# An attention layer on one core: new slot table with gaps, other order of the first steps, later clears, an earlier end of the last groups

## The chip, the cores and the metric

The kernel runs on one core of one Trainium2 chip. The metric is device time of one execution in microseconds. Engines are called by name: TensorE (PE in the rows, PEld for its weight loads), VectorE (DVE), ScalarE (ACT), GpSimd (POOL), SyncE (SP, which issues the DMAs). L12 is line 12 of the kernel.

## The reference, cut to what matters

```
x: (8, 1024, 256); 16 heads of 16; c = softplus(log_c); beta = softplus(beta)
h = layernorm(x);  q, k, v = h @ W.T, each mapped to the Poincare ball (exp_map)
dist = arccosh(max(1 + 2c*|q-k|^2 / ((1-c|q|^2)(1-c|k|^2)), 1+EPS)) / sqrt(c)
w = softmax(-beta*dist - bias);  o = w @ log_map(v);  o = log_map(exp_map(o))
x = x + o @ W_o.T
x = x + bf16(fp8_gemm(bf16(layernorm(x)), kernel)) + bias
```

Nearly all of the work is the 8 x 16 x 1024 x 1024 distances: a logarithm and a power of each.

## The kernel before, in words

**Tiles.** The 8192 tokens are 16 groups of 512 queries (G; in the tables the number n). Each group (counted from 0) takes 32 steps (`STEPS`): 4 sets of four heads, and in each 8 key tiles of 128. So n runs over 512 steps. A step has, on TensorE, the distances of four heads (`distances`, L1081; its two halves belong to two different coming steps) and the weights times values (`values`, L1096); on ScalarE a logarithm of 128x2048 numbers out of PSUM (Ln, L1192) and an exponential (Exp, L1199, the power of the step before). `distances(n + 1, second)` waits until Ln of step n has freed the shared banks. U is a ring of four buffers.

**Two paths.** Every unit of four steps reads a flag in a register and takes one of two branches. In the rare one VectorE bounds and clamps first (L1259, L1268) and Ln works on the result (L1187). In this data three units do, in groups 5, 8 and 15.

**The work between.** Projections of coming groups and the finish of past ones are cut into pieces and put into steps by a table written by hand. All pieces share PSUM bank 7: TensorE fills it, VectorE copies it out, and the next piece waits for that. `PROJECT_USES` and `FINISH_USES` say in which slot a piece stands and in which half: 0 (before `values`), 1 (after) or BOTH (split around it). Kinds: X turns the normalised input, M is a projection (four rows of L398 each), R turns scaled rows of queries or keys, A the largest values for the flags; T, W turn the attention's output and multiply it by W_o, Q and Y are the 8-bit product. S, every eighth step from step 10 (`SUM_STEPS`), turns the sums and has VectorE normalise them (L1282 to L1286). For groups from 3 on, slot k stands in step k - 4; for group 2 (`SECOND_USES`) in step k of group 0; for group 1, `FIRST_USES` names the steps of group 0. The finish of a group stands in the next group, the last but one uses `SHORT_USES`. VectorE's own arithmetic has slots too (`vector`, with its counts in `OWN`).

**Unread products.** A step with no piece gets two products (L1119, `keep_busy`) that nobody reads, one in each half.

**Start.** Groups 0 and 1 are projected before the loop through six PSUM banks (`FIRST_FILLS`); ScalarE copies. `first_vector` does VectorE's part for both. GpSimd clears `rows` and part of `vals` (`pool_zero`).

**End.** After the last step `last_tensor`, `last_scalar`, `last_vector` finish the last group. Then VectorE works out whether the fast path held; a flag is summed on TensorE and copied; after the block every engine loads it into a register and branches around the general path, which this data doesn't take.

## Time and profile before

| | us |
|---|---|
| three runs | 2004.28, 2000.06, 1993.87 |
| median | 2000.06 |
| profiled execution | 2002.46 |
| its span | 2000.7 |
| ScalarE busy | 1874.2 (94%) |
| TensorE busy | 1804.3 (90%) |
| VectorE busy | 1140.0 (57%) |
| mean granted TensorE clock | 0.972 |

Instructions of one engine overlap a little, so that 512 Ln and Exp of 1.92 and 1.96 us take less than their sum. The distance between the starts of two Ln is the length of a step.

### The profile page before, as it was taken

What the parts mean: (1) busy time and instruction counts of PE and PEld (TensorE: products, weight loads), DVE (VectorE), ACT (ScalarE), POOL (GpSimd) and SP (SyncE); (2) the same over time, 40 slices, a digit from 0 to 9 for tenths busy, and PEclk for the clock granted to TensorE, in tenths of its full rate; (3) what the DMA queues carried; (4) which work ended last, traced back from release to release, by engine and by line L of the source; (5) the groups of instructions that cost most, each with busy time, mean ns of one, the idle gap of its engine ahead of it and who ended that gap; (6) DMA issues with size and microseconds to landing.
All of it is one profiled execution on the core that took longest, in us unless ns stands there. A gap on an engine that the chain in (4) does not pass through costs nothing.

```text
span 2000.7 us, 29621 instructions
## 1 busy us (share of the span) xinstructions
PE 1804.3 (90%) x10753; PEld 609.2 (30%) x10753; DVE 1140.0 (57%) x2825; ACT 1874.2 (94%) x1094; POOL 14.5 (1%) x35
## 2 busy tenths in 40 slices
PE   7988989999898798989998898998989899999997
PEld 4222322323232232322322232232323223333334
DVE  7463565655566665665657656555655656322545
ACT  5789999999999699999998899999999999999992
POOL 2000000000000000000000000000000000000000
PEclk9699999999999899999999899999999999999997
DMA  1314113131312213122040320414122131311110
GB/s 56 111 68 124 54 64 96 38 133 43 112 43 81 73 43 112 44 100 75 22 133 22 102 74 24 131 43 133 40 94 65 43 102 44 122 43 43 43 33 22
DMA packets 112952, 142.53 MB, mean 71 GB/s; under 512 B 35691, under 2 KB 61548, under 8 KB 112748
## 3 DMA queue, kind: packets, MB, share of 16 engines
q1 hardware_dynamic: 112748, 140.13, 21.8%
q8 instruction: 89, 1.46, 0.3%
q14 instruction: 115, 0.94, 0.2%
HBM read 85.07 MB, written 55.05 MB: 70 GB/s over the span
## 4 chain that ended last, share of the span: by engine, by line
ACT 47%; PE 32%; issue 13%; DVE 5%; ACTq 3%; DMA 0%; DVEq 0%; SPq 0%
ACT U L1192 25%; ACT U L1199 22%; PE ps L1081 10%; PE ps L398 9%; PE ps L1096 8%; PE ps L688 3%; ACTq L1240 2%; DVE U L1268 1%; PE ps L1119 1%; DVE U L1259 1%; PE ps L403 0%; DMA U<-in_L_attn_W_o_dram 0%; DVE ss L532 0%; PE ps L394 0%; PE ps L168 0%
## 5 line engine op out<-in xcount | busy, mean ns | idle before, releaser
L1199 ACT ACTIVATE U<-U 128x2048 f32<-128x2048 f32 x512 | 1002.6, 1960 | 0.3
L1192 ACT ACTIVATE U<-ps 128x2048 f32<-128x2048 f32 x500 | 961.3, 1923 | 37.8 <-PE ps L1081 31.1
L1081 PE MATMUL ps<-q_T,k_T 18*128 18x512 f32 x4096 | 632.9, 650 | 133.5 <-ACT U L1192 108.1
L1096 PE MATMUL ps<-U,vals 128*32 128x512 f32 x4096 | 561.2, 620 | 27.6 <-ACT U L1199 27.3
L1081 PEld LDWEIGHTS ps<-q_T,k_T 18*128 18x128 f32 x4096 | 196.8, 186 | 349.3 <-ACT U L1192 270.4
L398 PE MATMUL ps<-wT,xnT 128*128 128x384 f32 x512 | 230.9, 543 | 4.8 <-DVEq L1292 2.5
L487 DVE COPY qkv<-ps 128x384 f32<-128x384 f32 x112 | 62.5, 558 | 221.0 <-PE ps L398 221.0
L1119 PE MATMUL ps<-woT,ident 128*128 128x256 f32 x396 | 141.7, 441 | 0.0
L1096 PEld LDWEIGHTS ps<-U,vals 128*32 128x32 f32 x4096 | 81.5, 109 | 197.5 <-ACT U L1199 133.6
L398 PEld LDWEIGHTS ps<-wT,xnT 128*128 128x128 f32 x512 | 80.7, 192 | 196.6 <-issue 112.1
L495 DVE COPY q_T<-ps 128x512 f32<-128x512 f32 x60 | 41.5, 692 | 124.3 <-PE ps L403 124.3
L403 PE MATMUL ps<-ident,rows 128*128 128x128 f32 x512 | 108.3, 308 | 3.3 <-DVEq L1292 1.7
L403 PEld LDWEIGHTS ps<-ident,rows 128*128 128x128 f32 x512 | 55.0, 146 | 181.1 <-issue 133.1
L1119 PEld LDWEIGHTS ps<-woT,ident 128*128 128x128 f32 x396 | 60.5, 192 | 162.3 <-issue 147.8
L1274 DVE COPY OTs<-ps 128x512 f32<-128x512 f32 x64 | 43.8, 684 | 73.1 <-PE ps L1096 73.1
L497 DVE COPY k_T<-ps 128x512 f32<-128x512 f32 x60 | 41.5, 692 | 70.7 <-PE ps L403 70.5
L688 PE MATMUL ps<-woT,fi_ocT 128*128 128x256 f32 x240 | 67.8, 405 | 0.0
L1282 DVE TENSOR_REDUCE den<-ps 128x16 f32<-128x256 f32 x64 | 27.2, 424 | 70.4 <-PE ps L1105 69.8
L688 PEld LDWEIGHTS ps<-woT,fi_ocT 128*128 128x128 f32 x240 | 40.6, 189 | 51.0 <-issue 25.2
L578 DVE TENSOR_REDUCE ss<-sqr 128x48 f32<-128x768 f32 x56 | 53.4, 953 | 1.9
L716 DVE TENSOR_TENSOR fi_x<-fi_xt,ps 128x512 f32<-128x512 f32 x30 | 20.6, 688 | 57.1 <-PE ps L688 57.1
L577 DVE TENSOR_TENSOR sqr<-qkv 128x768 f32<-128x768 f32 x56 | 53.1, 948 | 0.0
(209 smaller groups left out, 1177.8 us busy)
## 6 DMA issues: line engine op xcount, KB each, us to landing
rqb<-q_scratch SPq DMA_DIRECT2D x64, 1024.0 KB, 5.6
q_scratch<-q_T SPq DMA_DIRECT2D x16, 1024.0 KB, 4.5
k_scratch<-k_T SPq DMA_DIRECT2D x16, 1024.0 KB, 6.8
v_scratch<-vals SPq DMA_DIRECT2D x16, 768.0 KB, 9.5
fi_xt<-in_L_attn_x_dram SPq DMA_DIRECT2D x17, 512.0 KB, 5.2
xt<-in_L_attn_x_dram SPq DMA_DIRECT2D x15, 512.0 KB, 6.0
out_dram<-fi_x SPq DMA_DIRECT2D x15, 512.0 KB, 3.4
rk_scratch<-rk SPq DMA_DIRECT2D x16, 32.0 KB, 11.5
```

The lines of the kernel that those rows point to most:

```text
L398: ins = pe.matmul(bank[:, 0:384], xnT[:, dc, t * P:(t + 1) * P], g.wT[:, dc, half * 384:(half + 1) * 384], start=dc == 0, stop=dc == 1)
L403: ins = pe.transpose(bank[:, t * P:(t + 1) * P], rows[:, qk, t, hg * HPG:(hg + 1) * HPG, :].rearrange("p h r -> p (h r)"), g.ident[:, :])
L487: v.tensor_copy(qkv[:, t, 24 * half:24 * (half + 1), :].rearrange("p h d -> p (h d)"), bank[:, 0:384]).then_inc(a.b7_copied, 1)
L577: step(v.tensor_tensor(sqr[:, :], src, src, ALU.mult))
L578: step(v.tensor_reduce(ss[:, t, :], sqr[:, :].rearrange("p (h d) -> p h d", d=DH), AX.X, ALU.add))
L688: ins = pe.matmul(bank[:, a * D:(a + 1) * D], ocT[:, dc, t * P:(t + 1) * P], g.woT[:, dc, :], start=dc == 0, stop=dc == 1)
L1081: ins = pe.matmul(g.ps[:, 2 * pair + i, :], a.k_T[HB * h:HB * h + RD, b % 2, hg, kt * P:(kt + 1) * P], a.q_T[HB * h:HB * h + RD, G % 3, hg ...
L1096: ins = pe.matmul(g.ps[HB * h:HB * h + VW, 6, :], a.vals[:, b % 2, kt, (hg * HPG + h) // 2, DH * (h % 2):DH * (h % 2) + VW], U[:, n % RING ...
L1119: pe.matmul(g.ps[:, 7, 0:D], g.ident[:, :], g.woT[:, 0, :], start=True, stop=True)
L1192: act.activation(U[:, n % RING].rearrange("p b n -> p (b n)"), chunk(n), ACT.Ln, scale=-2.0 / EPS, bias=1.0).then_inc(freed, 1)
L1199: act.activation(U[:, n % RING], U[:, n % RING], ACT.Exp, scale=exponent).then_inc(exp_done, 1)
L1274: v.tensor_copy(OTs[:, :], g.ps[:, 6, :]).then_inc(ot_done, 1)
```

## The change

- **Table.** M4 to M7 move one slot back, so that slots 11 and 14 are empty; the pieces T, W of the finish move one slot back and W1 two (T 13, 14; W 15, 17). VectorE's slots from the third sum of squares on move one back, as does the projection's small exponential on ScalarE (slot 20 to 21); so do the finish's from 20 on. Step 7 (`BARE`) gets no unread products.
- **Group 2.** R pieces stand in 25 to 31 instead of 24 to 31.
- **First steps.** In step 0 TensorE waits for the last start copy and does five unread products. A0, R4, A1 of group 1 stand in that order in step 2, half 0. R7 and R0 stand in steps 11 and 14. VectorE scales only group 1's keys before the loop and its queries in step 3.
- **Clears.** GpSimd waits for VectorE's first normalised input, and clears only the part of `rows` that is not written later.
- **Last two groups.** `SHORT_SLOTS` packs the finish of group 14: Q in step 25, Y0 and Y1 in step 27, the residual in 28, the store in 29. Before: Q 27, Y 28, residual 29, store 30. The last group's transposes get eleven unread products after them instead of eight.
- **Flag.** VectorE's four operations of the flag stand after its copy of the last transposes, TensorE's sum behind the products with W_o, the copy behind the largest values; each engine loads the flag before the block ends.

Left out below: the renumbered slots in `vector` of both stages, and the callers that pass the new arguments.

```diff
@@ -51,26 +51,28 @@
                 ("M", 0): (7, BOTH), ("M", 1): (8, BOTH), ("M", 2): (9, BOTH), ("M", 3): (10, BOTH),
-                ("M", 4): (11, BOTH), ("M", 5): (12, BOTH), ("M", 6): (13, BOTH), ("M", 7): (15, BOTH),
+                ("M", 4): (12, BOTH), ("M", 5): (13, BOTH), ("M", 6): (15, BOTH), ("M", 7): (16, BOTH),
                 ("R", 0): (25, BOTH), ("R", 1): (26, BOTH), ("R", 2): (27, 0), ("A", 0): (27, 1),
...
 TOLD = 12
-FINISH_USES = {("T", 0): (12, BOTH), ("T", 1): (13, BOTH), ("W", 0): (14, BOTH), ("W", 1): (15, BOTH),
+FINISH_USES = {("T", 0): (13, BOTH), ("T", 1): (14, BOTH), ("W", 0): (15, BOTH), ("W", 1): (17, BOTH),
                ("Q", 0): (30, BOTH), ("Y", 0): (31, 0), ("Y", 1): (31, 1)}
...
 SHORT_USES = dict(FINISH_USES)
-SHORT_USES.update({("Q", 0): (27, BOTH), ("Y", 0): (28, 0), ("Y", 1): (28, 1)})
+SHORT_USES.update({("Q", 0): (28, BOTH), ("Y", 0): (30, 0), ("Y", 1): (30, 1)})
+BARE = 7
+SHORT_SLOTS = {23: (23, 24), 24: (25, 26), 25: (27, 28), 26: (29,), 27: (30, 31), 28: (32,), 29: (33,), 30: (), 31: ()}
 SUM_STEPS = 10
...
-FIRST_USES = {("R", 4): (2, 0), ("A", 0): (2, 0), ("A", 1): (2, 1), ("R", 5): (3, BOTH), ("R", 6): (6, BOTH),
-              ("R", 7): (14, BOTH), ("R", 0): (16, BOTH), ("R", 1): (17, BOTH), ("R", 2): (19, BOTH),
+FIRST_USES = {("A", 0): (2, 0), ("R", 4): (2, 0), ("A", 1): (2, 0), ("R", 5): (3, BOTH), ("R", 6): (6, BOTH),
+              ("R", 7): (11, BOTH), ("R", 0): (14, BOTH), ("R", 1): (17, BOTH), ("R", 2): (19, BOTH),
               ("R", 3): (20, BOTH)}
...
 SECOND_USES = dict(PROJECT_USES)
-SECOND_USES.update({("R", i): (24 + i, 0 if i in (3, 6) else BOTH) for i in range(8)})
-SECOND_USES.update({("A", 0): (27, 1), ("A", 1): (30, 1)})
+SECOND_USES.update({("R", 0): (25, BOTH), ("R", 1): (26, BOTH), ("R", 2): (27, 0), ("A", 0): (27, 1), ("R", 3): (28, 0),
+                    ("R", 4): (28, 1), ("R", 5): (29, BOTH), ("R", 6): (30, 0), ("A", 1): (30, 1), ("R", 7): (31, BOTH)})
@@ -338,13 +340,14 @@
-    OWN = {0: 9, 1: 10, 9: 2, 11: 2, 13: 2, 16: 3, 17: 4, 18: 6, 19: 2, 20: 6, 21: 5, 22: 4}
+    OWN = {0: 9, 1: 10, 9: 2, 11: 2, 14: 2, 17: 3, 18: 4, 19: 6, 20: 2, 21: 6, 22: 5, 23: 4}
     PER = sum(OWN.values())
...
         step = Steps(pool, zeroed, 0)
-        step(pool.memset(rows[:, :, :, :, :], 0.0))
+        pool.wait_ge(xn_rdy, 1)
+        step(pool.memset(rows[:, :, :, :, DH:], 0.0))
         step(pool.memset(a.vals[:, :, :, :, DH:VW], 0.0))
@@ -533,17 +536,24 @@
         step(v.tensor_scalar(ss[:, :, :], ss[:, :, :], EPS * EPS, None, ALU.max))
-        vector(v, n, 17, step)
         vector(v, n, 18, step)
+        vector(v, n, 19, step)
         if n == 0:
             v.wait_ge(zeroed, ZEROED)
-        vector(v, n, 19, step)
         vector(v, n, 20, step)
         vector(v, n, 21, step)
+        vector(v, n, 22, step)
         if n == 1:
             v.wait_ge(p_filled, len(FIRST_FILLS))
-        vector(v, n, 22, step)
         vector(v, n, 23, step)
+        scale_rows(v, n, (1, 0) if n == 0 else (1,))
+
+    def scale_rows(v, n, which):
+
+        for qk in which:
+            v.tensor_tensor(rows[:, qk, :, :, 0:DH], qkv_of(n)[:, :, qk * H:(qk + 1) * H, :],
+                            f[:, :, qk * H:(qk + 1) * H].unsqueeze(3).broadcast_to([P, GT, H, DH]),
+                            ALU.mult).then_inc(rows_rdy, 1)
@@ -617,17 +627,14 @@
             v.tensor_reduce(amax[:, :], a4[:, :, :].rearrange("p t h -> p h t"), AX.X, ALU.max).then_inc(amax_rdy, 1)
-        if k == 23:
-            for qk in (1, 0):
-                v.tensor_tensor(rows[:, qk, :, :, 0:DH], qkv[:, :, qk * H:(qk + 1) * H, :],
-                                f[:, :, qk * H:(qk + 1) * H].unsqueeze(3).broadcast_to([P, GT, H, DH]),
-                                ALU.mult).then_inc(rows_rdy, 1)
+        if k == 24:
+            scale_rows(v, n, (1, 0))
         assert first or step.n == OWN.get(k, 0), (k, step.n)
...
     p.first_sync, p.first_tensor, p.first_largest, p.await_largest = first_sync, first_tensor, first_largest, await_largest
-    p.first_scalar, p.first_vector, p.p_steps = first_scalar, first_vector, p_steps
+    p.first_scalar, p.first_vector, p.p_steps, p.scale_rows = first_scalar, first_vector, p_steps, scale_rows
     p.v_rdy, p.p_copied = v_rdy, p_copied
@@ -655,13 +662,13 @@
     psb = g.ps[:, 7, :].bitcast(BF16)
-    OWN = {3: 1, 4: 2, 6: 11, 20: 9, 21: 10, 22: 4, 23: 2, 24: 2, 27: 2, 32: 1}
+    OWN = {3: 1, 4: 2, 6: 11, 21: 9, 22: 10, 23: 4, 24: 2, 25: 2, 28: 2, 32: 1}
     PER = sum(OWN.values())
...
             if n >= 1:
-                sp.wait_ge(steps_v, PER * (n - 1) + sum(count for slot, count in OWN.items() if slot <= 27))
+                sp.wait_ge(steps_v, PER * (n - 1) + sum(count for slot, count in OWN.items() if slot <= 28))
             sp.dma_start(xt[:, :, :], g.x_g[n]).then_inc(f_in, 16)
@@ -786,6 +793,8 @@
         step = Steps(v, l_steps, sum(count for slot, count in LAST_OWN.items() if slot < k))
+        if k == 27:
+            v.wait_ge(xq_rdy, LAST)
         last_heads(v, step, slice(0, TOLD), [k])
@@ -807,14 +816,15 @@
-    def last_sync(sp):
+    def last_sync(sp, await_flag):
         for half in range(2):
...
             sp.dma_start(g.out_g[LAST][:, two, :], x1[:, two, :]).then_inc(res_out, 16)
+        await_flag(sp, "sync")
         sp.wait_ge(res_out, 16 * (NG + 1))
...
-    def last_tensor(pe, keep_busy):
+    def last_tensor(pe, keep_busy, flag_sum):
         def turn(i, banks):
@@ -822,7 +832,7 @@
         turn(0, (0, 0))
-        keep_busy(5, 8)
+        keep_busy(5, 11)
         pe.wait_ge(l_scaled, 2)
@@ -965,7 +978,7 @@
             slots = [(n, STEPS * (G - 1 - n) + s) for n in range(LAST - 1)]
-            slots += [(LAST - 1, k) for k in {29: (29, 32), 30: (30, 33)}.get(s, (s,)) if G == LAST]
+            slots += [(LAST - 1, k) for k in SHORT_SLOTS.get(s, (s,)) if G == LAST]
             return [(n, k) for n, k in slots if 0 <= k < FINISH_SLOTS]
@@ -1013,6 +1026,12 @@
+        def await_flag(eng, name):
+
+            eng.wait_ge(max_steps, 5)
+            g.needed[name] = eng.value_load(g.flag[0:1, 0:1], min_val=0, max_val=2 * P)
+
+        g.needed = {}
         with nc.Block() as block:
@@ -1147,9 +1170,12 @@
                         use(*key, 0)
-                    unused = n > 2 and not in_step(G, s, 0) + in_step(G, s, 1)
+                    unused = n > 2 and s != BARE and not in_step(G, s, 0) + in_step(G, s, 1)
                     if unused:
                         keep_busy(first_use[n])
+                    if n == 0:
+                        pe.wait_ge(project.p_copied, len(FIRST_FILLS))
+                        keep_busy_again(7, 5)
                     if n >= 1:
@@ -1159,14 +1185,13 @@
-                def keep_busy_again(bank, times):
-                    for _ in range(times):
-                        pe.matmul(g.ps[:, bank, 0:D], g.ident[:, :], g.woT[:, 0, :], start=True, stop=True)
                 pe.wait_ge(freed, N)
-                finish.last_tensor(pe, keep_busy_again)
-                pe.wait_ge(max_steps, 4)
-                pe.wait_ge(a.b7_copied, len(uses.place))
-                pe.matmul(g.ps[0:1, 7, 0:1], red[:, 0:1], ones_c[:, :], start=True, stop=True).then_inc(flag_ps, 1)
+
+                def flag_sum(pe):
+                    pe.wait_ge(max_steps, 4)
+                    pe.matmul(g.ps[0:1, 0, 0:1], red[:, 0:1], ones_c[:, :], start=True, stop=True).then_inc(flag_ps, 1)
+                finish.last_tensor(pe, keep_busy_again, flag_sum)
+                await_flag(pe, "tensor")
@@ -1317,6 +1343,8 @@
                             finish.last_early(v, s)
+                        if n == QUERY_STEP:
+                            project.scale_rows(v, 1, (0,))
                         if n == KERNEL_STEP:
@@ -1413,9 +1446,8 @@
-        def steps(eng, body, stored=None, ahead=None, again=None):
-            needed = eng.value_load(g.flag[0:1, 0:1], min_val=0, max_val=2 * P)
-            with eng.If(needed > 0):
+        def steps(eng, name, body, stored=None, ahead=None, again=None):
+            with eng.If(g.needed[name] > 0):
                 if ahead is not None:
```

`largest_weight` holds the four operations that stood behind `last_vector` (L1350 to L1355), `general_flag` the wait and the copy (L1356, L1357).

## Rows read from the trace of the kernel before

**Rows 1.** The page's costliest groups: line, shapes, count, busy us, mean ns, idle before.

```profile
L1192 ACT ACTIVATE U<-ps 128x2048 f32<-128x2048 f32 x500 | 961.3, 1923 | 37.8 <-PE ps L1081 31.1
```

**Rows 2.** Busy time by stage: PE, PEld, DVE, ACT, POOL, then granted clock, DMA.

```profile
300.67:416.59 115.92, 106.41 (x661) 34.73 (x658) 68.72 (x170) 115.16 (x67) 0.00 (x0) 1.00 0.23 76
...
60.00:70.00 10.00, 9.21 (x36) 2.49 (x36) 5.08 (x18) 4.70 (x4) 0.00 (x0) 0.50 0.43 109
...
165.30:169.00 3.70, 3.70 (x20) 1.16 (x20) 0.69 (x1) 1.77 (x1) 0.00 (x0) 0.62 0.00 0
```

**Rows 3.** Timeline of group 2, ScalarE: start us, us, operation, [idle before].

```profile
351.62 1.89 ACT L1192 ACTIVATE U<-ps 128x2048 f32<-128x2048 f32 x1
...
355.18 1.89 ACT L1192 ACTIVATE U<-ps 128x2048 f32<-128x2048 f32 x1
...
359.03 1.88 ACT L1192 ACTIVATE U<-ps 128x2048 f32<-128x2048 f32 x1 [0.15 <-PE ps L1081]
...
363.21 1.88 ACT L1192 ACTIVATE U<-ps 128x2048 f32<-128x2048 f32 x1 [0.22 <-PE ps L1081]
```

**Rows 4.** Timeline of group 2, TensorE: distances (L1081) and values (L1096).

```profile
321.00 1.14 PE L1081 MATMUL ps<-q_T,k_T 18*128 18x512 f32 x8
...
324.75 1.14 PE L1081 MATMUL ps<-q_T,k_T 18*128 18x512 f32 x8
...
359.98 1.07 PE L1096 MATMUL ps<-U,vals 128*32 128x512 f32 x8
...
362.04 1.14 PE L1081 MATMUL ps<-q_T,k_T 18*128 18x512 f32 x8
...
365.37 1.14 PE L1081 MATMUL ps<-q_T,k_T 18*128 18x512 f32 x8
```

**Rows 5.** Timeline of the first steps.

```profile
55.43 1.24 PE L1081 MATMUL ps<-q_T,k_T 18*128 18x512 f32 x8 [2.59 <-ACT U L1192]
...
59.56 2.36 DVE L622 TENSOR_TENSOR rows<-k_T,f 128x1024 f32<-128x1024 f32 x2
...
69.71 1.88 ACT L1192 ACTIVATE U<-ps 128x2048 f32<-128x2048 f32 x1 [4.82 <-PE ps L1081]
...
89.30 1.88 ACT L1192 ACTIVATE U<-ps 128x2048 f32<-128x2048 f32 x1 [0.20 <-PE ps L1081]
```

**Rows 6.** Timeline of step 26 of the first group.

```profile
165.29 0.44 PE L403 MATMUL ps<-ident,rows 128*128 128x128 f32 x2 [1.72 <-DVEq L1292]
...
169.85 1.88 ACT L1192 ACTIVATE U<-ps 128x2048 f32<-128x2048 f32 x1 [2.78 <-PE ps L1081]
```

**Rows 7.** Timeline of the last group's end.

```profile
1932.42 0.70 PE L1119 MATMUL ps<-woT,ident 128*128 128x256 f32 x2
...
1933.21 1.22 DVE L766 TENSOR_TENSOR fi_xq<-fi_ocT,fi_osq 128x1024 bf16<-128x1024 f32 x1
...
1949.41 1.88 ACT L1192 ACTIVATE U<-ps 128x2048 f32<-128x2048 f32 x1 [2.14 <-PE ps L1081]
...
1955.62 1.88 ACT L1192 ACTIVATE U<-ps 128x2048 f32<-128x2048 f32 x1 [2.54 <-PE ps L1081]
...
1965.51 3.62 PE L1164 MATMUL ps<-woT,ident 128*128 128x256 f32 x16
...
1970.95 0.66 PE L820 MATMUL ps<-ident,fi_osq 128*128 128x128 f32 x4 [1.82 <-DVE fi_osq L807]
...
1972.12 5.23 PE L832 MATMUL ps<-woT,fi_ocT 128*128 128x256 f32 x16 [0.52 <-DVE fi_ocT L869]
```

**Rows 8.** Timeline of the start, GpSimd and VectorE.

```profile
7.31 1.83 DVE L259 TENSOR_SCALAR rstd<-veps 128x4 int32<-128x4 int32 x1
...
7.31 1.81 POOL L348 MEMSET vals<- 128x2048 f32 x1
...
22.00 0.20 DVE L259 TENSOR_SCALAR rstd<-veps 128x4 int32<-128x4 int32 x1
```

**Rows 9.** The instructions of the line that loads the flag.

```profile
L1417 PEldq TENSOR_LOAD <-flag x1: 487/487/487, 1995.5 to 1995.5; - x1
```

More of the change, by code:

```diff
@@ L523, in scalar @@
     def scalar(act, n, k):
-        if k == 20:
+        if k == 21:
             act.wait_ge(n_rdy, n + 1)
@@ L572, in vector @@
             ins.then_inc(xn_rdy, 1)
[L573 to L574 removed]
+        if k in (9, 11, 14, 17):
+            t = {9: 0, 11: 1, 14: 2, 17: 3}[k]
             v.wait_ge(a.b7_copied, uses.after(("M", n, 2 * t + 1)))
@@ L834, in last_tensor @@
             ins.then_inc(l_filled, 1)
+        flag_sum(pe)
         pe.wait_ge(l_act, 2)
@@ L1049, in _ @@
                         project.sync(sp, m, k)
-                finish.last_sync(sp)
+                finish.last_sync(sp, await_flag)
                 sp.wait_ge(a.stored, 64 * NG)
@@ L1119, in keep_busy, with keep_busy_again @@
                     pe.matmul(g.ps[:, 7, 0:D], g.ident[:, :], g.woT[:, 0, :], start=True, stop=True)
+                def keep_busy_again(bank, times):
+                    for _ in range(times):
+                        pe.matmul(g.ps[:, bank, 0:D], g.ident[:, :], g.woT[:, 0, :], start=True, stop=True)
                 setup.tensor(pe)
@@ L1246, in _ @@
                 finish.last_scalar(act)
+                await_flag(act, "scalar")
             @block.vector
@@ L1344, in _, with largest_weight, general_flag @@
                         unit(n0, False)
+                def largest_weight():
+                    v.wait_ge(past_rdy, 1)
+                    v.tensor_scalar(red[:, 1:2], g.NEGB, -EXPONENT_MAX / THETA_MAX, None, ALU.is_lt).then_inc(max_steps, 1)
+                    v.tensor_reduce(red[:, 0:1], cm[:, :], AX.X, ALU.max).then_inc(max_steps, 1)
+                    v.wait_ge(max_steps, 2)
+                    v.tensor_scalar(red[:, 0:1], red[:, 0:1], past[:, :], None, ALU.is_gt).then_inc(max_steps, 1)
+                    v.wait_ge(max_steps, 3)
+                    v.tensor_tensor(red[:, 0:1], red[:, 0:1], red[:, 1:2], ALU.add).then_inc(max_steps, 1)
+                def general_flag():
+                    v.wait_ge(flag_ps, 1)
+                    v.tensor_copy(g.flag[:, :], g.ps[0:1, 0, 0:1]).then_inc(max_steps, 1)
                 copy_sums(NG * HG - 1)
                 normalise(LAST, HG - 1)
[L1347 to L1357 removed]
+                finish.last_vector(v, largest_weight, general_flag)
+                await_flag(v, "vector")
 def finish_again(nc, ctx, g):
@@ L1453, in _ @@
                 sp.sem_inc(gout, 16)
-                steps(sp, body, gout, again=again_sync)
+                steps(sp, "sync", body, gout, again=again_sync)
             @block.tensor
@@ L1476, in body @@
                     ins.then_inc(p_rdy, 1)
-                steps(pe, body, again=again_tensor)
+                steps(pe, "tensor", body, again=again_tensor)
             @block.scalar
@@ L1493, in body @@
                     act.activation(Z[:, :], X[:, :], ACT.Exp, scale=g.NEGB, bias=shift[:, :]).then_inc(a_rdy, 1)
-                steps(act, body, ahead=ahead)
+                steps(act, "scalar", body, ahead=ahead)
             @block.vector
@@ L1535, in body @@
                     v.tensor_scalar(Og[:, :], g.ps[:, 7, 0:DH], rsum[:, :], None, ALU.mult).then_inc(v_rdy, 1)
-                steps(v, body, ahead=ahead, again=again_vector)
+                steps(v, "vector", body, ahead=ahead, again=again_vector)
 def layer_kernel(nc, x, W_q, W_k, W_v, W_o, log_c, beta, attention_bias, ffn_w, input_scale, kernel_scale,
```

50 lines of the change are left out of this document (20 added, 30 removed).

## Prediction, made before the changed kernel was run

> **What bounds the kernel now.** I read the page's costliest groups first, then busy time by stage, then each engine in order of time around every place where Ln waits. ScalarE does two 128x2048 activations per step, a logarithm (Ln) of 1.92 us and an exponential (Exp) like it [rows 1], in 512 steps. In group 2 (counted from 0, 32 steps) it is busy 115.16 of 115.92 us and TensorE 106.41 [rows 2]: ScalarE is the bound and TensorE stands close behind it. Two Ln in a row start 351.62 and 355.18, 3.56 us apart (3.555 where I follow more of them), and nothing can shorten that. So 512 x 3.555 = 1820 us is fixed; the other 180 are the head, the tail, and the places where Ln waits.
>
> Where Ln waits, it waits for the distance products of TensorE. Those of the next chunk start when the Ln before ends, and Ln can start 1.18 us after they do (362.04 to 363.21) [rows 3, 4]. TensorE may thus run about 0.45 us late before ScalarE loses anything (3.56 less 1.88 less 1.2). It falls behind where a step carries more than 3.555 us of products: a step with a projection piece M takes 3.75 (321.00 to 324.75), one with two unread products 3.33 (362.04 to 365.37) [rows 4], one with a W piece 4.19 (the Ln that wait for two of them are 4.18 apart, 359.03 to 363.21) [rows 3]. A group costs 115.92 - 113.76 = 2.16 us above the floor: 0.29 + 0.63 after the two W steps (3.85 and 4.18 us between the Ln) [rows 3], and the other 1.2 after the seven M steps in a row. 13 groups have this. The other losses are single places: some 25 us in the first group, the three units of four steps that take the exact path (34 together), and the end.
>
> **The new table, groups 1 to 13.** M pieces now stand in steps 3 to 6, 8, 9, 11, 12 of a group; step 7 has no piece and no unread product, and W0, W1 stand in 15 and 17. An M step adds 0.195 us of lateness (0.28 the first, out of idle), and ScalarE pays what exceeds 0.45. Four in a row cost about 0.56 instead of 1.15. In the bare step TensorE has 1.14 + 1.07 us of work (distances, values) [rows 4] in 3.56, so it catches up wholly; the pairs after it cost about 0.04 each. W0: 0.05 + 0.74 - 0.49 = 0.30. The step between has two unread products and gives back 3.56 - 3.33 = 0.23. The projection's small Exp, so far hidden in the wait for W1, moves one step and now stands open: 0.30. W1 then adds 0.15. Sum 1.38 against 2.16: 0.8 a group, 10 us in 13 (bounds 0 and 15: all of the M and W terms stay, or go), 0.5 in group 14, 0.5 for the same M steps in group 0. The sum-of-exponents piece S in step 10 stays apart from M, as before. VectorE's pieces move by one slot each; it is at 57% and the rows it scales in slot 24 are wanted at 25, with some 2 us to spare.
>
> **First steps.** TensorE idles 2.59 us before 55.43 [rows 5] and shortly after the granted clock falls: 60 to 70 us has 0.50, that is 1.2 instead of 2.4 GHz [rows 2]. Until 88 us everything on TensorE takes double, and Ln 4 starts only at 69.71 after a wait of 4.82, Ln 8 at 89.30. The change puts five unread products there. Sixteen rows (eight products) take 3.62 us [rows 7], so five take 2.2 and end near 55.0, before the Ln that frees the bank ends: hidden at 2.4 GHz, up to 1.9 us late at 1.2. Also VectorE scales only the keys before the loop (half of 2.36 us [rows 5]), so A0, R4, A1, now together ahead of the distances of step 4, come 1.2 us sooner; the query half runs in step 3, where VectorE has 3.3 us idle. Retimed at full clock: R4 at 61.2, A1 at 62.8, values to 64.6, the other half of step 4's distances then, Ln 4 at 65.8: 3.9 us won. From there four steps take 14.2 instead of 19.59: 5.4 more. Together 9.2 at most; where the clock still falls, the three pieces ahead of the distances cost 0.4, so the range is -0.4 to +9.2. I take 7.
>
> This is where a rule bears. By the Trainium skill (TensorE: Matmul & The Clock Gate, Part 1) the unit that judges TensorE's activity is free-running and not aligned with the kernel's start. The trace has the clock at 0.62 from 165.30 to 169.00 [rows 2], right after 1.72 us idle [rows 6]. By the rule the same gap may pass in one execution and cost in the next; by the rows alone each gap of this size costs each time. The first would leave a part of the 9.2 to luck.
>
> **Stalls that stay.** Group 2's pieces use the slot number as the step, so M3 still meets S in step 10, and now R1 instead of R2 meets S in step 26: the piece behind S waits until VectorE has read the bank, TensorE idles, Ln waits 2.78 there [rows 6]. No gain.
>
> **GpSimd.** The two large clears stood beside VectorE's first statistics: the 0.20 us operation of 22.00 took 1.83 at 7.31, beside the clear of vals that also starts at 7.31 [rows 8]; a second one lost 0.5. After the move VectorE has its rows 2.1 us earlier, but TensorE is in order behind the weight transposes until 12.4, so 0.1 is won. The clears now stand beside the constants' small operations at 12.5 to 16, behind which the first group's sums of squares wait; VectorE idles 1.1 us there. Bounds: +0.1 and, if the whole 1.8 us clear is waited for, -0.7. I take +0.1. The Trainium skill (SBUF — State Buffer, its terms) says that VectorE and GpSimd hold their shared port pair for a whole instruction and that the loser fully blocks; the trace agrees (1.83 for 1.81), and by that rule the -0.7 is what the move risks.
>
> **The end.** Y0 and Y1 stood in step 28. VectorE came late (it loads its branch flag between the units of four), TensorE idled over 2 us, the clock fell, and Ln 510 and 511 waited 2.14 and 2.54 [rows 7]. Their spacings are 5.91 and 6.21, 5.0 above the floor. Now Y is in step 27 and steps 28 to 31 carry unread products only: 5.0 gone. The last values finish nearer to their Exp at full clock: 1.4 more, so 6.4. But Q0 moves to step 25, and what it reads is written only at 1934.43 (1933.21 + 1.22), since both slots 25 and 26 stand behind the copy of the sums in step 24. TensorE is ready for it at 1932.42 [rows 7]. It idles 2.1 us, and values and the next products queue behind it: Ln 507 1.1 us late, and with a clock fall as after the 1.72 us gap up to 3.7. I take 2.
>
> Eleven unread products instead of eight last 5.0 us instead of 3.62, from 1965.51 to 1970.5, just inside the gap before 1970.95 [rows 7]. If this holds the clock, the 16 rows of L832 at 1972.12 (5.23 us, the first part at half clock) give 1.5; I take 1. The four small operations of the flag stand after the copy at 1971.64, where VectorE waits 2.27 us: free, and if not, 0.7. The flag's copy and wait cost 0.2 on VectorE's last chain. Loading the flag inside the block removes 0.49 + 0.17 + their gaps, 0.94 us, from behind the last barrier [rows 9]; on SyncE it hides in the wait for the last store.
>
> **Sum.** 10 + 0.5 + 0.5 + 7 + 0.1 + 6.4 - 2 + 1 - 0.2 + 0.9 = 24.2. The exact-path units lose an M in step 7 and a W, and have the scaled rows inside one of them: 0, bounds -3 and +3. The profiled execution took 2002.46 us (span 2000.7 and 1.8 around it), 2.4 above the median of 2000.06 of three runs that lie 10 us apart. 2002.46 - 24.2 = 1978.3; I say 1978, 1.1% below the median.
>
> **Rivals.**
> - The first steps' clock falls all the same. For it: the gap at 56.7 to 57.2 and the one before 59 stay, and TensorE is under two thirds busy there. Against it: the longest gap is filled. 1978 + 7.4 = about 1986.
> - The table gives nothing, because another piece becomes late: VectorE in slots 18 to 24 with its moved rows, or the small Exp in the open. For it: TensorE's total per group is unchanged. Against: the losses sit exactly where pieces are in a row. 1988.
> - The tail's new stall at Q0 takes its full 3.7 and the fall of the clock repeats near the last transposes: 1983.
> - Slower: the bare step lets the clock fall. Where there is no backlog TensorE is 62% busy in it, gaps of 0.6 and 0.7. The fall after 165.29 made Ln 3.7 us late (2.78 of them a wait [rows 6]) where I retime the stall alone at 1.3, so some 2.4. In all 15 groups that is 36: 1978 + 36 = 2014. It decides from about 9 groups on. Against it: in steps with S the gap is 0.7 too and the granted clock of that group is 1.00 [rows 2]; with M behind it the bare step has only one gap.
>
> **How the numbers follow.** Forecast 0.5, first-steps rival 0.22, table 0.11, tail 0.1, bare step 0.07. The forecast's own range is 1970 to 1986; with the rivals and the bounds 1967 to 1993 holds 8 in 10. A change of 0.5% (10 us) is about what a measurement here can tell from none; faster by more 0.86, within 0.07, slower 0.07.
>
> **What would show it.** Right: Ln spacings of 3.75 only at steps 5 to 7 of a group, one of about 3.86 at 17, a group of 115.1 us; granted clock 1.00 from 50 to 100 us and Ln 8 near 80; no wait before the last two Ln, but one near step 25 of the last group; end within 5 us of the last store's landing. Wrong: groups still of 115.9, a clock under 1 in step 7, or Ln 4 near 70.

## The result and the profile after

The changed kernel takes 1988.78 us (median of 21 runs, 1985.24 to 1994.75); the kernel before, beside it on the same chip, 1997.10 (21 runs, 1990.19 to 2005.27). The ratio is 0.9961 with a 95% interval of 0.9948 to 0.9973: 8 us or 0.4% faster. The forecast was 1978 (1967 to 1993) and 22 us. The time lies inside the range, but little more than a third of the gain is there. A second comparison on another occasion gave 1987.11 and 0.9942 (0.9922 to 0.9962), so by the two ratios the change is worth 8 to 12 us.

The profiled execution took 1994.49 us, its span is 1992.7 (before 2002.46 and 2000.7), and the mean granted clock 0.972 as before. The group of the logarithm, answers to [rows 1]: its idle time is 35.5 us instead of 37.8.

```profile
L1217 ACT ACTIVATE U<-ps 128x2048 f32<-128x2048 f32 x500 | 955.7, 1911 | 35.5 <-PE ps L1100 31.6
```

The stages show more. Group 2 answers to [rows 2]: 115.14 us instead of 115.92. The other windows are the first steps, the bare step of group 14, the bare step of group 15 and what follows it, and the steps behind the new stall at Q0. Columns are those of [rows 2].

```profile
300.44:415.58 115.14, 105.09 (x657) 34.06 (x654) 69.05 (x170) 114.84 (x67) 0.00 (x0) 1.00 0.25 77
60.00:70.00 10.00, 8.08 (x34) 2.11 (x30) 6.90 (x33) 6.25 (x4) 0.00 (x0) 0.72 0.50 154
1735.00:1748.00 13.00, 11.60 (x72) 3.65 (x68) 1.82 (x2) 13.00 (x9) 0.00 (x0) 1.00 0.00 0
1850.00:1856.00 6.00, 4.67 (x32) 1.36 (x35) 0.00 (x0) 6.00 (x5) 0.00 (x0) 1.00 0.00 0
1856.40:1866.70 10.30, 10.30 (x39) 2.44 (x31) 1.82 (x2) 7.58 (x5) 0.00 (x0) 0.51 0.01 2
1931.50:1941.70 10.20, 10.20 (x45) 2.81 (x44) 4.23 (x9) 7.01 (x5) 0.00 (x0) 0.50 0.20 54
```

The timeline of ScalarE, from group 2 to the end, with TensorE's and VectorE's instructions that explain the waits. 357.98 to 365.67 are the W steps of [rows 3]; 324.51 to 331.36 the M steps and the bare step, to be read against [rows 4]; 55.34 to 89.01 the first steps of [rows 5]; the rest the last group and the end, [rows 7].

```profile
55.34 2.43 PE L1142 MATMUL ps<-woT,ident 128*128 128x256 f32 x10
...
60.95 1.13 PE L1100 MATMUL ps<-q_T,k_T 18*128 18x512 f32 x4 [0.70 <-ACT U L1217]
...
62.72 0.66 PE L406 MATMUL ps<-ident,rows 128*128 128x128 f32 x4 [0.43 <-DVEq L505]
...
64.16 0.18 PE L414 MATMUL ps<-ident,amax_r 32*1 32x32 f32 x1 [0.78 <-DVE k_T L500]
...
70.22 1.88 ACT L1217 ACTIVATE U<-ps 128x2048 f32<-128x2048 f32 x1 [3.97 <-PE ps L1100]
...
89.01 1.87 ACT L1217 ACTIVATE U<-ps 128x2048 f32<-128x2048 f32 x1
...
324.51 1.14 PE L1100 MATMUL ps<-q_T,k_T 18*128 18x512 f32 x8
...
328.26 1.14 PE L1100 MATMUL ps<-q_T,k_T 18*128 18x512 f32 x8
...
331.36 1.24 PE L1100 MATMUL ps<-q_T,k_T 18*128 18x512 f32 x8 [0.89 <-ACT U L1217]
...
357.98 1.88 ACT L1217 ACTIVATE U<-ps 128x2048 f32<-128x2048 f32 x1
...
361.80 1.88 ACT L1217 ACTIVATE U<-ps 128x2048 f32<-128x2048 f32 x1
...
365.67 1.87 ACT L1217 ACTIVATE U<-ps 128x2048 f32<-128x2048 f32 x1
...
1739.30 1.07 PE L1115 MATMUL ps<-U,vals 128*32 128x512 f32 x8 [0.56 <-ACT U L1224]
1741.07 1.24 PE L1100 MATMUL ps<-q_T,k_T 18*128 18x512 f32 x8 [0.70 <-ACT U L1217]
...
1854.03 1.07 PE L1115 MATMUL ps<-U,vals 128*32 128x512 f32 x8 [0.56 <-ACT U L1224]
1855.80 1.81 PE L1100 MATMUL ps<-q_T,k_T 18*128 18x512 f32 x8 [0.70 <-ACT U L1217]
...
1863.83 1.88 ACT L1217 ACTIVATE U<-ps 128x2048 f32<-128x2048 f32 x1 [2.72 <-PE ps L1100]
...
1868.50 1.88 ACT L1217 ACTIVATE U<-ps 128x2048 f32<-128x2048 f32 x1 [0.99 <-PE ps L1100]
...
1928.65 1.23 DVE L773 TENSOR_TENSOR fi_xq<-fi_ocT,fi_osq 128x1024 bf16<-128x1024 f32 x1
...
1930.03 0.38 PE L700 MATMUL ps<-ident_b,fi_xq 128*128 128x128 bf16 x4 [2.09 <-DVE fi_xq L773]
...
1933.95 1.88 ACT L1217 ACTIVATE U<-ps 128x2048 f32<-128x2048 f32 x1 [1.93 <-PE ps L1100]
...
1950.47 1.88 ACT L1217 ACTIVATE U<-ps 128x2048 f32<-128x2048 f32 x1
...
1958.87 4.92 PE L1142 MATMUL ps<-woT,ident 128*128 128x256 f32 x22
1964.32 0.65 PE L830 MATMUL ps<-ident,fi_osq 128*128 128x128 f32 x4 [0.53 <-DVE fi_osq L816]
1965.48 3.72 PE L842 MATMUL ps<-woT,fi_ocT 128*128 128x256 f32 x16 [0.52 <-DVE fi_ocT L880]
```

The two spans differ by 8.0 us. From the starts of the first Ln of each group this is where they went:

| stretch | before | after | difference |
|---|---|---|---|
| start to the first Ln | 46.2 | 47.3 | +1.1 |
| group 0 | 138.6 | 138.0 | -0.7 |
| groups 1 to 13 | 1535.80 | 1525.24 | -10.56 |
| group 14 | 114.96 | 114.73 | -0.23 |
| group 15, first to last Ln | 120.0 | 125.2 | +5.2 |
| last Ln to the end | 45.1 | 42.2 | -2.8 |

The last group is the surprise: it was to lose 3 us (5 gone at Y, 2 added at Q0) and gained 5. Its steps from 8 to 16 take 3.72, 6.41, 4.67, 7.24, 3.91, 4.65, 4.51, 1.82, 5.25 us from the start of one Ln to the next, where before the long ones begin at 11 (7.07, 3.91, 5.11, 4.50, 1.82, 3.67; steps 12 to 15 are the exact path's, and the 1.82 is its last step, whose Exp comes after the next Ln); steps 26 to 28 take 5.65, 4.93, 4.46; the last two take 3.56 each instead of 5.91 and 6.21.

### The profile page after: what moved, and what is told of

Read it like the earlier page. It is cut to its first block, busy times and chain, and to the rows that moved or that the text cites. A ratio compares the mean times of both kernels' runs of the same rounds, so it can differ in the third digit from the quotient of the medians.

```text
span 1992.7 us, 29554 instructions
## 1 busy us (share of the span) xinstructions
PE 1788.6 (90%) x10713; PEld 603.1 (30%) x10713; DVE 1142.9 (57%) x2825; ACT 1869.9 (94%) x1094; POOL 12.8 (1%) x35
## 4 chain that ended last, share of the span: by engine, by line
ACT 54%; PE 24%; issue 14%; DVE 4%; ACTq 3%; DMA 0%; DVEq 0%; SPq 0%
ACT U L1217 28%; ACT U L1224 26%; PE ps L1100 8%; PE ps L401 6%; PE ps L1115 5%; ACTq L1265 2%; PE ps L695 2%; DVE U L1294 1%; PE ps L1138 1%; PE ps L406 1%; PE ps L1142 1%; DVE U L1285 1%; DVE rows L554 0%; DMA U<-in_L_attn_W_o_dram 0%; ACT e L529 0%
## 5 line engine op out<-in xcount | busy, mean ns | idle before, releaser
L1217 ACT ACTIVATE U<-ps 128x2048 f32<-128x2048 f32 x500 | 955.7, 1911 | 35.5 <-PE ps L1100 31.6
L1138 PE MATMUL ps<-woT,ident 128*128 128x256 f32 x340 | 121.8, 441 | 3.8 <-DVEq L1318 3.6
L1138 PEld LDWEIGHTS ps<-woT,ident 128*128 128x128 f32 x340 | 52.0, 193 | 145.2 <-issue 116.0
```

The costliest lines, as they stand in the source:

```text
L1138: pe.matmul(g.ps[:, 7, 0:D], g.ident[:, :], g.woT[:, 0, :], start=True, stop=True)
L1217: act.activation(U[:, n % RING].rearrange("p b n -> p (b n)"), chunk(n), ACT.Ln, scale=-2.0 / EPS, bias=1.0).then_inc(freed, 1)
```

## Experiments

All are variants of the changed kernel. Ratios are to the kernel before, run beside them (medians 2000.89, 1995.98, 1998.43 and 1998.12 us in the four comparisons). "Both" means the bare step filled in groups 14 and 15 and Q0's input in time; the three rows that begin with "with" are edits of the version without a piece behind S. The last column is the time from the first to the last Ln of group 15, less 31 steps of 3.555 us (110.2), in one execution of each.

| kernel | median us | ratio | 95% interval | group 15 above its floor, us |
|---|---|---|---|---|
| after, again | 1987.11 | 0.9942 | 0.9922 to 0.9962 | 15.0 |
| bare step filled in groups 14, 15 | 1980.41 | 0.9899 | 0.9880 to 0.9917 | 7.4 |
| Q0's input in time | 1986.20 | 0.9925 | 0.9907 to 0.9942 | 10.7 |
| both | 1981.41 | 0.9904 | 0.9888 to 0.9921 | 4.8 |
| both, again | 1981.22 | 0.9914 | 0.9895 to 0.9932 | 4.8 |
| both, old first steps | 1982.95 | 0.9929 | 0.9914 to 0.9944 | 4.8 |
| both, tighter first steps | 1978.06 | 0.9906 | 0.9890 to 0.9922 | 4.8 |
| both, no piece behind S | 1972.75 | 0.9881 | 0.9861 to 0.9902 | 4.7 |
| the same, again | 1973.81 | 0.9883 | 0.9864 to 0.9901 | 4.7 |
| with products in every step 7 | 1975.50 | 0.9887 | 0.9868 to 0.9906 | 6.3 |
| with eight products at the end | 1977.69 | 0.9892 | 0.9875 to 0.9910 | 4.8 |
| with step 16 bare too | 1978.11 | 0.9893 | 0.9874 to 0.9913 | 7.2 |
| table alone | 1986.95 | 0.9944 | 0.9929 to 0.9960 | 7.8 |
| no piece behind S, old first steps | 1974.33 | 0.9890 | 0.9873 to 0.9906 | 4.8 |

### The changed kernel once more

> The changed kernel again, as the yardstick for the three beside it. Both theories: 1988.8 us median as in the 21 executions so far, ratio to the kernel before 0.996; executions in two clusters near 1987 and 1994. The profile read so far has all of the table's gain (13 groups of 115.14 instead of 115.92 us), so the rest must be lost elsewhere.

Group 15 repeats to 0.1 us in every spacing (3.75, 6.41, 4.62, 7.24 from step 8; 5.70, 4.93, 4.45 from 26), with the low clock at 1850.3 to 1860.6 and 1925.4 to 1935.7. Only the start differs: the first Ln comes at 45.5 us instead of 47.3, and group 0 takes 133.9 us instead of 138.0. The losses of the last group came back in both executions; those of the first group vary. The times of single executions of this one kernel lie up to 10 us apart (1983.91 to 1993.85), so a term of 2 us can be read from rows that repeat but not from medians.

### The bare step filled in the last two groups

```diff
-                    unused = n > 2 and s != BARE and not in_step(G, s, 0) + in_step(G, s, 1)
+                    unused = n > 2 and (s != BARE or G >= LAST - 1) and not in_step(G, s, 0) + in_step(G, s, 1)
```

> Step 7 keeps its two unread products in groups 14 and 15, where no projection piece stands beside it; it stays bare in groups 1 to 13. Theory (the bare step drops the clock only where nothing is late behind it): the 5 us lost in steps 8 to 11 of the last group go, the cluster near 1994 goes, median 1986 and a spread of 3 us or less. Rival (that fall was one of chance, as many others): median and clusters as the changed kernel, 1989 and 1994.

It is 6.7 us faster than the changed kernel beside it, and the intervals of the two ratios don't touch. The small spread that was expected with it did not come: the four executions lie between 1978.56 and 1986.16. The granted clock is 1.00 throughout steps 8 to 10. On ScalarE's timeline the Ln of steps 8, 9 and 10 stand 3.56 us apart (3.72 and 6.41 in the changed kernel):

```profile
1852.92 2.04 ACT L1217 ACTIVATE U<-ps 128x2048 f32<-128x2048 f32 x1
...
1856.48 2.05 ACT L1217 ACTIVATE U<-ps 128x2048 f32<-128x2048 f32 x1
...
1860.04 2.06 ACT L1217 ACTIVATE U<-ps 128x2048 f32<-128x2048 f32 x1
```

Group 14 takes 114.73 us with the products and without them. So two unread products in one step of 512, step 7 of group 15, are worth 6 to 8 us. This is the largest single cause of the shortfall.

### Q0's input in time

```diff
-SHORT_SLOTS = {23: (23, 24), 24: (25, 26), 25: (27, 28), 26: (29,), 27: (30, 31), ...
+SHORT_SLOTS = {23: (23, 24, 25, 26), 24: (27,), 25: (28,), 26: (29,), 27: (30, 31), ...
```

> The 8-bit input of group 14 is worked out in step 23, ahead of the copy of the sums in step 24, so that Q0 in step 25 finds it ready. Theory (the 2.09 us stall before Q0 and the clock that falls after it cost 4.4 us in steps 26 to 28): the stall goes, steps 26 to 31 take 3.56 each, 4 us less than the changed kernel, 1985. Rival (the stall is absorbed and the fall comes anyway, from Y0 and Y1): 1 us or nothing, 1988.

VectorE now writes Q0's input one step earlier. The wait of 2.09 us is gone; in the timeline, TensorE's Q0 and two Ln of ScalarE at the floor:

```profile
1928.36 0.40 PE L700 MATMUL ps<-ident_b,fi_xq 128*128 128x128 bf16 x4
...
1932.34 1.93 ACT L1217 ACTIVATE U<-ps 128x2048 f32<-128x2048 f32 x1
...
1935.90 1.94 ACT L1217 ACTIVATE U<-ps 128x2048 f32<-128x2048 f32 x1
```

The last group loses 4.4 us less. The median moved by 0.9 and the ratio by 0.0017 (3.4 us), with overlapping intervals: shown in the rows, not in the time.

> Both edits: unread products in step 7 of groups 14 and 15, and the 8-bit input in step 23. Theory: the two add up, since they stand in different steps, 1982 us, 0.7% below the kernel before. Rival (the clock's falls come by chance and move elsewhere): no better than the better of the two alone.

With both edits the last group stands 4.8 us above its floor. The four cells 15.0, 7.4, 10.7, 4.8, one execution each, are not a plain sum: the bare step costs 7.6 where the stall is there and 5.9 where it isn't, the stall 4.4 or 2.6. The rows say where the difference lies. The 2.1 us wait before Q0 is there with the bare step filled too, but the clock is then low for 3.4 us (1923.8 to 1927.2) and only step 26 is long (6.14 us), while in the changed kernel it is low for 10.2 us and three steps are long. The median is no better than that of the first edit alone (1981.41 and 1980.41): that the second edit gains anything on top is shown in the rows only.

### The first steps undone

> The kernel with both edits of the last study again (unread products in step 7 of groups 14 and 15, 8-bit input in step 23), as the yardstick of this study. Both theories: 1981 us, ratio to the kernel before 0.990; its profile had 1973.9 us of span with a quick first group, so the spread comes from the first 180 us.

```diff
-FIRST_USES = {("A", 0): (2, 0), ("R", 4): (2, 0), ("A", 1): (2, 0), ...
+FIRST_USES = {("R", 4): (2, 0), ("A", 0): (2, 0), ("A", 1): (2, 1), ...
-                    if n == 0:
-                        pe.wait_ge(project.p_copied, len(FIRST_FILLS))
-                        keep_busy_again(7, 5)
```

(and both scaled rows before the loop, as before the change)

> The kernel with both edits, but its first steps as in the kernel before: no five unread products in step 0, R4, A0 in half 0 and A1 in half 1 of step 2, both halves of group 1's rows scaled before the loop. Theory (the new first steps win next to nothing, since the clock still falls near 60 us after the waits around A0, R4 and A1): within 3 us of the yardstick. Rival (as I forecast: 7 us of the gain are theirs): 7 us slower than the yardstick, 1988.

The old first steps are slower by 1.7 us in the medians and 3 in the ratios (the intervals overlap), and by 0.8 us in group 0 of the two profiles (138.65 and 137.82). One group 0 says little, because the same code had given 132.2 us in the first execution of "both". Over all profiles that have the meetings of pieces with S, group 0 takes 132.2 to 138.5 us with the new first steps (seven, mean 136.7) and 138.6 to 138.7 with the old (three). Busy time by stage, as in [rows 2] with the clock in the third column from the end, of the version with the new first steps:

```profile
50.00:60.00 10.00, 8.96 (x51) 4.63 (x49) 8.82 (x26) 9.21 (x9) 0.00 (x0) 0.91 0.61 219
60.00:70.00 10.00, 8.79 (x36) 2.23 (x36) 5.68 (x31) 6.00 (x5) 0.00 (x0) 0.60 0.35 81
70.00:80.00 10.00, 9.78 (x40) 2.59 (x40) 3.81 (x7) 6.84 (x5) 0.00 (x0) 0.50 0.63 204
```

And of the one with the old:

```profile
50.00:60.00 10.00, 8.04 (x41) 4.52 (x43) 9.41 (x30) 8.05 (x10) 0.00 (x0) 0.67 0.37 136
60.00:70.00 10.00, 9.22 (x34) 2.45 (x30) 3.61 (x6) 6.85 (x4) 0.00 (x0) 0.50 0.50 157
70.00:80.00 10.00, 8.38 (x40) 1.83 (x36) 6.51 (x33) 7.35 (x4) 0.00 (x0) 0.67 0.66 116
```

The five products push the fall back, they don't prevent it: it stands at 56.0 to 57.7 us in the four profiles with the old first steps and at 59.5 to 65.0 in the twelve with the new.

### The first steps tighter

```diff
-FIRST_USES = {("A", 0): (2, 0), ("R", 4): (2, 0), ("A", 1): (2, 0), ...
+FIRST_USES = {("A", 0): (2, 0), ("R", 4): (2, 0), ("A", 1): (2, 1), ...
+                    if n == 1:
+                        keep_busy_again(7, 1)
```

> The kernel with both edits, with A1 moved behind the values of step 2 and one more unread product behind the values of step 1, so that TensorE has no wait of 0.78 us before A1 and none of 0.70 before step 2. Theory (these short waits in a row make the clock fall near 60 us): the clock stays at full speed past 60 us, step 4's Ln starts by 67 instead of 70 us, the first group is 6 us shorter, 1975. Rival (the fall comes from the idle time before 57 us or by chance): as the yardstick, 1981.

The clock still falls at 64.6 us and stays low to 88.5; group 0 takes 138.3 us. Of the waits that the edit was to remove, the 0.70 us before 60.95 is gone, but one of 0.83 us still stands before the distances at 64.36. The median is 3 us lower, the intervals overlap, and the trace has no reason for it: inconclusive. That the three short waits from 60.95 to 64.16 cause the fall is not shown.

### No piece behind S in group 0

```diff
+SECOND_USES.update({("M", 3): (11, BOTH), ("R", 0): (25, 0), ("R", 1): (25, 1), ...
-              ("R", 7): (11, BOTH), ("R", 0): (14, BOTH), ("R", 1): (17, BOTH), ("R", 2): (19, BOTH),
-              ("R", 3): (20, BOTH)}
+              ("R", 7): (14, BOTH), ("R", 0): (17, BOTH), ("R", 1): (19, BOTH), ("R", 2): (20, BOTH),
+              ("R", 3): (21, BOTH)}
```

(SyncE's part for group 1 moves from step 21 to 22 with R3)

> The kernel with both edits, and no piece of group 2 behind S in steps 10 and 26: M3 of group 2 in step 11, R0 and R1 of group 2 in the two halves of step 25, group 1's R7, R0 to R3 in steps 14, 17, 19, 20, 21. Theory (each piece behind S idles TensorE by 1.7 to 2.5 us and brings the clock down): steps 11, 26, 27 take 3.6 instead of 6.9 to 8.5, 6.7 and 4.4 us, so 6 to 8 us less than the yardstick, 1974. Rival (the time comes back as late pieces in the fuller steps 25 and 11 to 14): 2 us or less.

> The kernel of the last study without pieces behind S, again, as the yardstick here (unread products in step 7 of groups 14 and 15, 8-bit input in step 23, group 2's M3 in 11, R0 and R1 in 25). Both theories: 1973 us, ratio to the kernel before 0.988.

In the changed kernel M3 of group 2 waits at step 10 until VectorE has read S from the bank, TensorE idles 2.50 us, the clock falls and Ln waits 5.93:

```profile
102.94 1.65 PE L401 MATMUL ps<-wT,xnT 128*128 128x384 f32 x2 [2.50 <-DVEq L1318]
...
109.50 1.88 ACT L1217 ACTIVATE U<-ps 128x2048 f32<-128x2048 f32 x1 [5.93 <-PE ps L1100]
```

With M3 one step later nothing waits; these are ScalarE's Ln of steps 12 and 13:

```profile
103.63 1.87 ACT L1217 ACTIVATE U<-ps 128x2048 f32<-128x2048 f32 x1
...
107.19 1.88 ACT L1217 ACTIVATE U<-ps 128x2048 f32<-128x2048 f32 x1
```

Group 0 takes 128.6 and 128.5 us in the two executions, and 126.5 to 131.8 in all those with this edit and the new first steps, instead of the 132 to 138 of the versions above. The ratios are 0.9881 and 0.9883: 23 to 25 us under the kernel before and 12 to 16 under the changed one. **This version beats both kernels.** The prediction named these two meetings under stalls that stay and priced no gain, which was right for the change; they were worth more than any edit to the start.

### Products in every step 7

```diff
-                    unused = n > 2 and (s != BARE or G >= LAST - 1) and not in_step(G, s, 0) + in_step(G, s, 1)
+                    unused = n > 2 and not in_step(G, s, 0) + in_step(G, s, 1)
```

> The yardstick with the two unread products kept in step 7 of all groups. Theory (the gap in the table wins because TensorE catches up wholly in the bare step; with products it gives back only 0.23 of the 0.49 us): the pair of M behind it loses 0.3 to 0.4 us more, a group takes 115.5 instead of 115.15, 4 to 5 us in 13 groups, 1977. Rival (an empty slot is enough, whatever TensorE does in it): no difference.

The pair of M behind step 7 now ends in one step of 3.69 us (212.20 to 215.89) where the bare step leaves 3.58. ScalarE's timeline with products in step 7:

```profile
212.20 1.88 ACT L1217 ACTIVATE U<-ps 128x2048 f32<-128x2048 f32 x1
...
215.89 1.88 ACT L1217 ACTIVATE U<-ps 128x2048 f32<-128x2048 f32 x1
```

And with the bare step:

```profile
212.16 1.88 ACT L1217 ACTIVATE U<-ps 128x2048 f32<-128x2048 f32 x1
...
215.74 1.88 ACT L1217 ACTIVATE U<-ps 128x2048 f32<-128x2048 f32 x1
```

Group 1 takes 115.30 instead of 115.17 us: 0.13 a group, where 0.3 to 0.4 had been expected. The empty slot does nearly all of the table's work, the missing products little. By this the products, kept everywhere, would have cost the change 13 x 0.13 = 1.7 us, as much as the two medians differ (within their intervals), and spared it 6 to 8. One execution is no proof of it: group 5 took 132.8 instead of 130.1 us in this one, and group 15, where nothing was edited, 1.6 us more.

### Eight products at the end

```diff
-        keep_busy(5, 11)
+        keep_busy(5, 8)
```

> The yardstick with eight unread products after the last group's first transposes, as before, instead of eleven. Theory (the eleven hold the clock through the products with W_o; in the trace before it was at half for 3.4 us there): 1 to 1.5 us slower, the clock low for one stretch near the end, the 16 rows of the products with W_o take 5.2 us again. Rival (with the rest of the end at full clock the gap of 1.8 us does no harm): no difference in the median or in those rows.

The wait before the last transposes is 1.81 us again, and the 16 rows of products with W_o take 5.32 instead of 3.72:

```profile
1941.21 3.62 PE L1142 MATMUL ps<-woT,ident 128*128 128x256 f32 x16
1946.65 0.66 PE L830 MATMUL ps<-ident,fi_osq 128*128 128x128 f32 x4 [1.81 <-DVE fi_osq L816]
1947.82 5.32 PE L842 MATMUL ps<-woT,fi_ocT 128*128 128x256 f32 x16 [0.52 <-DVE fi_ocT L880]
```

This term is shown in the rows, 1.6 us; the median moved by 3.9 with overlapping intervals.

### Step 16 bare too

```diff
-                    unused = n > 2 and (s != BARE or G >= LAST - 1) and not ...
+                    unused = n > 2 and (s not in (BARE, 16) or G >= LAST - 1) and not ...
```

> The yardstick with step 16, between W0 and W1, bare too in groups up to 13. Theory (the lateness model): TensorE comes out of the step with none of its 0.25 us, W1's step 18 spacing falls from 3.65 to 3.56, a group takes 115.0 instead of 115.15, 1 to 2 us in all; clock unchanged, because TensorE is still late when it enters the step. Rival (a second bare step lowers the clock in some groups): 2.4 us for each group in which it falls, slower than the yardstick.

The step between the W pieces gives back 0.07 to 0.1 us a group (115.10 against 115.17 in group 1, 115.05 against 115.14 in group 2), by a spacing of 3.56 instead of 3.65 at step 18. Against that, group 5 takes 133.1 instead of 130.1 and group 15 117.4 instead of 114.9, each with a longer low stretch of the clock, though nothing was edited in group 15. No gain.

### The table alone

All of the change but the table undone: the single clear, the old first steps, unread products in the bare step of groups 14 and 15, Q0 in step 27 and Y in 28, eight products at the end. The flag's operations stay moved.

```diff
-SHORT_SLOTS = {23: (23, 24), 24: (25, 26), 25: (27, 28), 26: (29,), 27: (30, 31), ...
+SHORT_SLOTS = {20: (20, 21), 21: (22,), 22: (23,), 23: (24,), 24: (25,), ... 28: (29, 30, 31), ...
-        keep_busy(5, 11)
+        keep_busy(5, 8)
```

> The change with its table, GpSimd order and start and end undone as far as they can be: the new table stays in all groups (pieces M in steps 3 to 6, 8, 9, 11, 12, W0 in 15, W1 in 17, the bare step 7 in the groups before 14 alone), and so do the shorter rows clear's absence of a wait, that is the old single clear, the old order of the first steps with no products at Ln 2 and both scaled rows before the loop, eight unread products at the end, Q0 in step 27 and Y0, Y1 in step 28; the flag's operations and its load stay where the change has them. Theory (the table is worth what was forecast for it, 0.78 us in each of 13 groups, and the rest of the change took about as much in the last group as it gave elsewhere): groups of 115.14 to 115.2 us, about 10 us below before, ratio 0.995, the stall of Ln 510 and 511 back (5 us above the floor), no fall of the clock after step 7 of group 15. Rival (other parts were needed for the gain, and the table moves other losses into groups 0 and 15): ratio 0.998 or more.

Busy time of its group 2:

```profile
299.94:415.02 115.08, 105.02 (x656) 33.99 (x654) 69.00 (x170) 114.78 (x66) 0.00 (x0) 1.00 0.25 77
```

The median has 0.9944, 11.2 us (8 to 14 by the interval): all that the whole change gives (0.9961 and 0.9942). So the other parts cancel, as the table of stretches says. Not all of it is the table's. In the profile groups 1 to 14 give 11.0 us; the last two spacings are 5.19 and 4.91 us, 2.0 less than in the kernel before though nothing was done for them, and the stretch behind the last Ln is 1.4 shorter, with the flag's operations moved. The clock does not fall after step 7 of group 15.

### The best version with the old first steps

> The version without the meetings of S with M and R (both last-group mends in it too), with the change's first steps undone: R4 before A0, A1 in the second slot, no five products behind Ln 2, both scaled rows before the loop. It is compared with that version's two medians, 24.3 us (ratio 0.9881) and 24.6 us (0.9883) below before. Theory (the new first steps move the fall of the clock by a few us and give 1 to 3 us): ratio 0.989 to 0.990, Ln 32 some 2 us later, the clock low already near 57 to 60 us in the trace. Rival (they give the 7 us of the forecast once nothing else in group 0 waits): ratio 0.9915 or more. Rival (they give nothing): 0.988.

The ratio is 0.9890 against 0.9881 and 0.9883: some 1.5 us, inside the intervals. Group 0 takes 128.56 us against 128.56 and 128.53. What the new first steps give is 0 to 3 us, not 7.

## Why the prediction was wrong, step by step

The forecast missed at two places, both on TensorE's clock: the 7 us for the first steps, and the bare step, whose cost the sum put at nothing. The stall at Q0 cost 2.4 us more than its 2. The table, the largest term, was right.

**The table: right.** "0.8 a group, 10 us in 13": 0.75 to 0.79 in nine of them (group 2: 115.14), 0.67 and 0.56 in groups 1 and 10, 0.9 and 1.4 in the exact-path groups 5 and 8, and 10.56 in all from group 1 to 13. Group 14 gave 0.23 where 0.5 was forecast. The spacings are those forecast: the distances of 324.51 and 328.26 stand 3.75 us apart, then TensorE idles 0.89 us in the bare step at 331.36 and has caught up; 3.82 and 3.87 us from 357.98 to 361.80 to 365.67, where [rows 3] have 3.85 and 4.18. The kernel with the table alone gives 11.2 us, 11.0 of them in these groups by its rows.

**First steps: "I take 7".** This failed; the first rival came in its place. At 55.34 the products fill what was the longest gap of [rows 5], but the clock falls at 64.3 instead of 56.9, Ln 4 starts at 70.22 (it was to start at 65.8), Ln 8 at 89.01 (forecast near 80). I had priced the removal of one gap as the removal of the fall, with a chance of 0.22 for the other outcome, although the shorter gaps and the busy share that spoke for it were in the text. Measured with two versions and their old first steps: 0 to 3 us. (The two parts of the 9.2 add up to 9.3.)

**Bare step: put at zero, and priced too low as a rival.** The rival asked for a fall in all groups and from nine on. It comes in one, the last, and there costs 5.9 to 7.6 us where I had 2.4. In groups 1 to 13 M stands behind the bare step, as I had argued. Groups 14 and 15 have none, and there the same two gaps, 0.56 and 0.70 us, stand in both: in group 14 (1739.30, 1741.07) the clock stays at 1.00, in group 15 (1854.03, 1855.80) it is 0.51 right after, and low at the same place in each of the three executions profiled with this step bare. A fall in a loop without slack costs more than the one late instruction: two Ln wait (2.72 and 0.99) and steps 8 to 10 lose 4.1 us. The rest stands further on, 1.6 of it at step 16 (5.25 us instead of 3.67), and is not shown to follow from this fall: the same 5.25 came in the version with products in every step 7, where nothing fell here. The error was to price a fall by one piece retimed, and to ask only whether a mechanism is general.

The Trainium skill (TensorE: Matmul & The Clock Gate, Part 1) says that the unit that judges the activity is free-running. By that rule the gaps alone don't decide whether the clock falls; the trace agrees, since the same pair passed in group 14 and cost in group 15. That it was group 15 each time, though this group started 6 us apart in two of them (1825.25 and 1819.29), no run here explains.

**Q0: the wait right, its cost too small.** "It idles 2.1 us": 2.09. The input was written at 1928.65 + 1.23, as read. But steps 26 to 28 stand 4.4 us above the floor, where I took 2 with an upper bound of 3.7: the clock is 0.50 from 1931.50 to 1941.70 and three Ln wait. With the bare step filled the same wait cost 2.6, near the forecast; what decides between the two, no run here shows.

**Y: right.** The last two steps are at the floor, 5.0 us gone. "The last values finish nearer to their Exp, 1.4": last Ln to the products with W_o took 16.50 us before (1955.62 to 1972.12 in [rows 7]) and takes 15.01 now, with the clock at 1.00 where it was 0.50 up to 1961.6. It takes 15.02 with the table alone too, where the clock is back before the last Ln, so that this is the clock's part and not the new place of Y.

**Eleven products: right, a little better.** 4.92 us long, 0.53 of wait behind them, 3.72 instead of 5.23 for the 16 rows: 1.5 where I took 1.

**Flag: 0.9 less 0.2, in this execution -0.15.** From the end of these products to the end of the span it is 23.35 us before and 23.50 after. VectorE's load now stands between its last operations (0.3), and the branch still comes 3.5 us after the last store is issued: before because the loads followed the barrier, now because the store landed late. In the eleven later profiles with Q0's input in time the last store lands 2.1 us after its issue and the branch follows at 2.6 or 2.7 us, so that the 0.9 comes; in the three others without that edit, as in this one, the store lands 2.7 to 3.1 us after its issue. Why the two go together, no run here explains.

**GpSimd and the start.** The 1.83 us operation of [rows 8] is gone from 7.31 (it takes 0.17 at 6.69). But a small operation at 12.70 that took 0.16 now takes 1.17, beside the clear of `vals` that starts at 12.04: the risk that was bounded by -0.7 came in another place, VectorE begins its next statistics only 0.3 us sooner (19.59 against 19.93), and the first Ln was not sooner for it. It starts between 45.1 and 47.6 us from one execution to the next with the same code at the start, more than this term could show.

**The sum again,** with what the runs showed: table -11, first steps -1.5, Y -5.0, values -1.5, last products -1.5, Q0 and the bare step together +10.3 (15.04 less 4.76): -10.2, where 8 to 12 were measured. Of the 14 us that are missing from 24.2, 5.5 are the first steps, 8.3 Q0 and the bare step (2 were forecast), and the rest is small.
